# Decoder layer on one core: self-attention scores from float32r halves kept on chip, in place of bfloat16 triples stacked through HBM

## The reference, cut to what matters

```python
# x: (4, 512, 256), 16 heads of 16 columns
q, k, v = x @ w_q.T, x @ w_k.T, x @ w_v.T            # heads split off
scores = einsum('bqhd,bkhd->bhqk', q, k) * 16 ** -0.5
out = einsum('bhqk,bkhd->bqhd', softmax(scores), v)
x = layernorm(x + out @ w_o.T)
x = layernorm(x + cross_attention(x, ctx))           # 64 context rows a batch
x = layernorm(x + mixture_of_experts(x))             # 8 experts, 2 a token
```

## Time and profile before

| | us |
|---|---|
| median of three runs (888.09 to 890.46) | 890.4 |
| the profiled execution | 889.74 |
| its span, first to last instruction | 888.0 |
| busy in it: PE, PEld | 686.3, 449.1 |
| busy in it: DVE, ACT, POOL | 349.9, 285.8, 212.3 |

### The profile page before, as it was taken

The page is one execution under the profiler, slowest core; times in us unless marked ns, Lnnn a source line. Parts: engine busy times, 40 slices in busy tenths (PEclk is TensorE's granted clock), DMA queues, the critical chain, the costliest instruction groups (busy, mean ns, idle before and its releaser), DMA issues.

```text
span 888.0 us, 13256 instructions
## 1 busy us (share of the span) xinstructions
PE 686.3 (77%) x4099; PEld 449.1 (51%) x4100; DVE 349.9 (39%) x750; ACT 285.8 (32%) x501; POOL 212.3 (24%) x265
## 2 busy tenths in 40 slices
PE   7572266999999986764677862099999999999980
PEld 3230111322222245541213652089999999999970
DVE  2252344888888546653443875000000000000004
ACT  3220133767666643332354211011111111111112
POOL 1020100111111122112111067213333333333322
PEclk9876786999999999886689995599999999999995
DMA  6999992000001430858713722356666566656615
GB/s 207 129 170 169 141 151 32 3 1 1 1 1 44 136 53 37 134 82 130 98 53 101 250 77 50 105 161 180 175 169 177 167 173 180 174 174 175 170 45 189
DMA packets 75777, 103.61 MB, mean 117 GB/s; under 512 B 15044, under 2 KB 60637, under 8 KB 75742
## 3 DMA queue, kind: packets, MB, share of 16 engines
q1 hardware_dynamic: 63006, 90.53, 45.0%
q0 software_dynamic: 8512, 8.44, 5.8%
q10 hardware_dynamic: 4224, 4.19, 1.7%
HBM read 82.95 MB, written 21.40 MB: 118 GB/s over the span
## 4 chain that ended last, share of the span: by engine, by line
PE 64%; DMA 14%; DVE 7%; SPq 5%; POOL 4%; issue 3%; ACT 2%; DVEq 0%; ACTq 0%; POOLq 0%
PE ps L1566 16%; PE ps L1577 15%; PE ps L1288 7%; DMA scrq<-parts 7%; PE ps L1297 7%; PE ps L1233 5%; SPq L393 3%; POOL metas L664 3%; DMA qst<-mT 3%; PE ps L1381 2%; PE ps L1454 2%; PE ps L1447 2%; DMA qst<-scr_q 1%; PE ps L1413 1%; DVE xr L993 1%
## 5 line engine op out<-in xcount | busy, mean ns | idle before, releaser
L890 DVE TENSOR_REDUCE nmx<-ps 128x1 f32<-128x512 f32 x256 | 160.4, 681 | 55.0 <-PE ps L1233 55.0
L745 ACT ACTIVATE probs<-ps 128x512 f32<-128x512 f32 x256 | 133.8, 606 | 93.7 <-PE ps L1288 93.6
L1566 PEld LDWEIGHTS ps<-xtT,w1c 128*128 128x128 f32 x1248 | 147.1, 194 | 4.3 <-issue 2.4
L1566 PE MATMUL ps<-xtT,w1c 128*128 128x128 f32 x1248 | 147.6, 277 | 1.8 <-ACT xtT L845 1.8
L1577 PE MATMUL ps<-wexp,hidT 128*128 x624 | 141.0, 379 | 0.0
L1198 DVE TENSOR_SCALAR yw<-ps,mt 128x256 f32<-128x256 f32 x39 | 18.9, 484 | 292.2 <-PE ps L1577 292.2
L1577 PEld LDWEIGHTS ps<-wexp,hidT 128*128 128x128 f32 x624 | 115.6, 190 | 14.2
L1288 PE MATMUL ps<-qst,kst 99*128 (+1 forms) x256 | 96.4, 396 | 33.9 <-DMA qst<-mT 31.8
L1233 PE MATMUL ps<-kst,qst 96*128 (+1 forms) x256 | 94.6, 396 | 33.6 <-DVE nmx L890 17.3
L851 ACT ACTIVATE hidT<-ps 128x1024 f32<-128x1024 f32 x39 | 40.0, 1024 | 229.8 <-PE ps L1566 229.8
L703 POOL DMA_INDIRECT acc<-yw,mt x39 | 61.7, 1582 | 172.0 <-DVE yw L1198 172.0
(11 more groups left out here) (162 smaller groups left out, 668.1 us busy)
## 6 DMA issues: line engine op xcount, KB each, us to landing
w1c<-in_w1T SPq DMA_DIRECT2D x39, 1024.0 KB
wexp<-in_w2T SPq DMA_DIRECT2D x8, 1024.0 KB, 5.5
qst<-scrq SPq DMA_DIRECT2D x24, 256.0 KB, 9.2
kst<-scrk SPq DMA_DIRECT2D x24, 256.0 KB, 19.7
qst<-scr_q SPq DMA_DIRECT2D x24, 256.0 KB, 8.8
scrq<-parts SPq DMA_DIRECT2D x4, 768.0 KB, 18.1
scrk<-parts SPq DMA_DIRECT2D x4, 768.0 KB, 18.6
scr_q<-parts SPq DMA_DIRECT2D x4, 768.0 KB, 3.4
```

The lines of the kernel that those rows point to most:

```text
L745: act.activation(probs[n % 8][:, :], ps[:, 4 + n % 3, :], ACT.Exp).then_inc(s_exp, 1)
L890: dve.tensor_reduce(nmx[j % 2][:, k:k + 1], ps[:, slot, :], AX.X, ALU.max, negate=True).then_inc(s_mfree, 1)
L1566: mm = pe.matmul(ps[:, 2 * (j % 2) + f // 4, f % 4 * P:(f % 4 + 1) * P], w1c[j % 2][:, k * FF + f * P:k * FF + (f + 1) * P], xtT[j % 2][:, ...
```

## The change

Queries and keys are no longer split in bfloat16 triples. ScalarE evicts each projection to float32r (the high number), VectorE the rest (the low number), in tiles that stay on chip. To have high and low numbers of one head on 32 partitions, the weight columns are doubled first (`wqd`, `wkd`), so that a projection gives one unit's four heads on 4 x 32 partitions. A score tile is then two float32r matmuls on one row group of 32 rows of the array (32 rows, then 16, or 18 with the two rows of the maxima), and the four heads of a unit lie on the four row groups. Each projection has 128 columns, so there are 40 of them (16 for q, 16 for k, 8 for v), where the front had 12 larger ones; 33 of them now stand between score tiles, at places that two tables give. The whole of self-attention is written out, with no loop. Maxima run 26 tiles ahead of the exponentials (`LEAD`) and have three PSUM banks where they had four. They are turned as float32, copied as a high and a low number by VectorE, and moved into `qb` by eight DMAs a unit; two more DMAs a unit write ones. GpSimd has no part in the units any more, and `vu` is written by ScalarE at the eviction of v. The loads for later stages stand behind single units' rows on SP's queue.

```diff
+LEAD = 26
+TURN_AT = 3
+
+
+HIGHS = 2 * HD
+MAX_ROWS = 2
+PROJECTIONS = ("q0", "k0", "q1", "k1", "v0", "q2", "k2", "v1", "q3", "k3")
...
+    qa, qb, ka, kb = ([sb(f"{n}{i}", S, F32R, R_Q) for i in range(2 * NU)] for n in ("qa", "qb", "ka", "kb"))
...
+    PROLOGUE = {1: "q1", 4: "k1", 8: "v0", 12: "q2", 16: "k2"}
+    FIRST_BATCH_AT = {2: "v1", 6: "q3", 11: "k3"}
+    NEXT_BATCH_AT = [dict(zip(at, PROJECTIONS)) for at in
+                     ((15, 20, 25, 30, 35, 41, 46, 51, 57, 62), (3, 9, 17, 23, 29, 35, 41, 47, 53, 59))]
...
-        def make_stacks(b):
-            for qk in range(2):
-                sp.wait_ge(s_p3, 2 * b + qk + 1)
-                sp.dma_start(scr[qk][ds(b, 1)].rearrange("b (m p) r t -> p (b m) (r t)", p=P),
-                             parts[qk][:, :].rearrange("p (m a) -> p m a", m=KD)).then_inc(s_st[qk], 16)
-            sp.wait_ge(s_stack, 192 * b)
-            for qk, stack, part in ((0, qst, Q_PART), (1, kst, K_PART)):
-                sp.wait_ge(s_st[qk], 16 * (b + 1))
-                for g, r in enumerate(part):
-                    sp.dma_start(stack[HD * g:HD * g + HD, ds(b * H * S, H * S)].rearrange("d (h t) -> d h t", h=H),
-                                 scr[qk][ds(b, 1), :, r].rearrange("b (h d) t -> d (b h) t", d=HD)).then_inc(s_stack, 16)
...
+        def ones_rows(u):
+            sp.wait_ge(s_kb, u + 1)
+            for r in range(HD, HD + MAX_ROWS):
+                sp.dma_start(kb[u % (2 * NU)][r:P:HIGHS, :].bitcast(F32).rearrange("p (a t) -> p a t", a=HG),
+                             onesr[:, :].unsqueeze(1).to_broadcast([HG, HG, S // HG])).then_inc(s_one[u % NU], 16)
+
+        def max_rows(w):
+            sp.wait_ge(s_mfree, turn_slot(w) + 1)
+            for r, m in ((HD, mT_hi), (HD + 1, mT_lo)):
+                for i in range(HG):
+                    sp.dma_start(qb[w % (2 * NU)][HIGHS * i + r:HIGHS * i + r + 1, :].bitcast(F32).rearrange("p (a t) -> p a t", t=P),
+                                 m[w % 2][QT * i:QT * (i + 1), :].bitcast(F32)).then_inc(s_mrow[w % 2], 16)
...
+        ones_rows(0)
+        for w in range(UNITS):
+            if w + 1 < UNITS:
+                ones_rows(w + 1)
+            max_rows(w)
+            if w in BEHIND_ROWS:
+                BEHIND_ROWS[w]()
...
+        def q_high(b, u, name):
+            act.wait_ge(s_proj, proj_number(b, name) + 1)
+            act.activation(qb[(NU * b + u) % (2 * NU)][:, :], ps[:, proj_bank(b, name), :], ACT.Copy).then_inc(s_qb, 1)
...
+        for e in range(UNITS * TILES):
+            act.wait_ge(s_e, e + 1)
+            if e % HG == 0 and e >= 8:
+                act.wait_ge(s_pv, e // HG - 1)
+            act.activation(probs[e % 8][:, :], ps[:, 3 + e % 3, :], ACT.Exp).then_inc(s_exp, 1)
+            for b, name in projections_at(e):
+                evict(b, name)
...
+            dve.tensor_copy(mT_hi[w % 2][:, :], ps[0:TILES, n % 3, 0:P]).then_inc(s_mhi, 1)
+            dve.wait_ge(s_mhi, w + 1)
+            dve.tensor_tensor(mT_lo[w % 2][:, :], ps[0:TILES, n % 3, 0:P], mT_hi[w % 2][:, :], ALU.subtract).then_inc(s_mfree, 1)
...
+        def q_both(b, u, name):
+
+            n = NU * b + u
+            dve.wait_ge(s_qb, n + 1)
+            dve.scalar_tensor_tensor(out=qa[n % (2 * NU)][:, :], in0=ps[:, proj_bank(b, name), :], scalar=not_low[:, 0:1],
+                                     in1=qb[n % (2 * NU)][:, :], op0=ALU.mult, op1=ALU.add).then_inc(s_qa, 1)
+
+        def k_low(b, u, name):
+            n = NU * b + u
+            dve.wait_ge(s_ka, n + 1)
+            dve.tensor_tensor(kb[n % (2 * NU)][:, :], ps[:, proj_bank(b, name), :], ka[n % (2 * NU)][:, :],
+                              ALU.subtract).then_inc(s_kb, 1)
...
-        def max_half(w, k, j):
-
-            h, qt = k // QT, k % QT
-            n = max_tile(w, k)
-            if not (isinstance(w, int) and n < 4):
-                pe.wait_ge(s_mfree, n - 3)
-            pe.matmul(ps[:, tile_slot(j, k, isinstance(w, int) and w == 0), :],
-                      qst[0:ROWS, ds((w * HG + h) * S + qt * P, P)],
-                      kst[0:ROWS, ds((w * HG + h) * S, S)], start=True, stop=True).then_inc(s_mready, 1)
-
-        def max_turn(w, j, last=False):
-            pe.wait_ge(s_m3, w + 3)
-            pe.wait_ge(s_mfree, max_turned(w, last) - 3)
-            pe.transpose(ps[:, j % 4, :].bitcast(BF16)[0:M3W, 0:P], m3[j % 2][:, :], identb[:, :]).then_inc(s_mready, 1)
...
+        def max_tile(w, k):
+            n, (qt, i) = max_slot(w, k), divmod(k, HG)
+            if k == 0:
+                pe.wait_ge(s_qa, w + 1)
+                pe.wait_ge(s_kb, w + 1)
+            if n >= 3:
+                pe.wait_ge(s_mfree, n - 2)
+            u, both, highs = w % (2 * NU), slice(HIGHS * i, HIGHS * (i + 1)), slice(HIGHS * i, HIGHS * i + HD)
+            pe.matmul(ps[:, n % 3, :], qa[u][both, qt * P:(qt + 1) * P], ka[u][both, :], start=True, stop=False)
+            pe.matmul(ps[:, n % 3, :], qb[u][highs, qt * P:(qt + 1) * P], kb[u][highs, :], start=False,
+                      stop=True).then_inc(s_mready, 1)
+
+        def max_turn(w):
+            n = turn_slot(w)
+            pe.wait_ge(s_mfree, max(max_slot(w, TILES - 1) + 1, n - 2))
+            pe.matmul(ps[0:TILES, n % 3, 0:P], nmx[w % 2][:, :], identf[:, :], start=True, stop=True).then_inc(s_mready, 1)
...
+                    mm = pe.matmul(ps[:, at, :], wd[:, (k * NU + i) * P:(k * NU + i + 1) * P],
+                                   xTb[b][:, k * S:(k + 1) * S], start=(k == 0), stop=(k == KD - 1))
...
-        def exp_tile(u, n):
-            kt, h = n // HG, n % HG
-            if n >= 3:
-                pe.wait_ge(s_exp, HG * QT * u + n - 2)
-            pe.matmul(ps[:, 4 + n % 3, :], kst[:, ds((u * HG + h) * S + kt * P, P)],
-                      qst[:, ds((u * HG + h) * S, S)], start=True, stop=True).then_inc(s_e, 1)
...
+        def exp_tile(e):
+            u, (kt, i) = e // TILES, divmod(e % TILES, HG)
+            if e % TILES == 0:
+                pe.wait_ge(s_mrow[u % 2], 16 * HG * MAX_ROWS * (u // 2 + 1))
+                pe.wait_ge(s_one[u % NU], 16 * MAX_ROWS * (u // NU + 1))
+            if e >= 3:
+                pe.wait_ge(s_exp, e - 2)
+            w, both, more = u % (2 * NU), slice(HIGHS * i, HIGHS * (i + 1)), slice(HIGHS * i, HIGHS * i + HD + MAX_ROWS)
+            pe.matmul(ps[:, 3 + e % 3, :], ka[w][both, kt * P:(kt + 1) * P], qa[w][both, :], start=True, stop=False)
+            pe.matmul(ps[:, 3 + e % 3, :], kb[w][more, kt * P:(kt + 1) * P], qb[w][more, :], start=False,
+                      stop=True).then_inc(s_e, 1)
...
+        for e in range(UNITS * TILES):
+            exp_tile(e)
+            maxima(e + LEAD)
+            if e % HG == 1 and e >= HG:
+                pv(e // HG - 1)
+            for b, name in projections_at(e):
+                project(b, name)
```

519 lines of the change are left out of this document (232 added, 287 removed).

## The result

The changed kernel takes 930.5 us (924.6 to 937.6, 4 runs) against 890.4 (888.1 to 893.8, 4 runs) of the kernel before on the same chip: ratio 1.045, 95% interval 1.036 to 1.054. The forecast was 873 us with a range of 846 to 915. Faster was expected, slower came, and the range missed it.

A forecast was written before the change was run, and what follows sets the result against it. From 141 us TensorE was nearly always busy, units taking 11.93 us. Self-attention: 39.5 + 167.2 + 66 + 4.5 + 26.0 + 4.4 = 307.6 us against 324.4, so 889.7 - 16.8 = 873 us, range 846 to 915.

The forecast's parts named there:

- The clock: Rival: gaps at waits bring TensorE to 1.2 GHz for four of sixteen units, 44 us more, 917 us; chance 0.07.
- 0.216 a pass: Score tiles on TensorE: each float32r matmul is one 0.216 us pass, four side by side, 3.5 us a unit.
- A unit's base: Self-attention units: 11.94 us each without projections, as before, plus 0.3 for the float32 turn of the maxima.
- the last two: Last two units of self-attention, without maxima: taken as unchanged, 26.0 us.
- The start: Front up to the first maxima tile: doubled weights, projections q and k of unit 0, evictions; 12.5 us.
- GpSimd loses work that nobody waited for: nothing: Units: taking GpSimd's work away was priced at no time.
- Four groups side by side: Score tiles: four row groups work at once and a waiting group doesn't hold up the next; 873 us, chance 0.50.
- one pass for a float32r matmul: Score tiles: low numbers are split off beforehand, so a float32r matmul streams once, 0.216 us.
- 2.0 us a projection: 33 projections between score tiles: 1.71 us each plus two changes of array shape at 0.15, 66 us in all.
- waits for the maxima rows: Heads of units 12 to 15: TensorE waits 1.1 us each, 4.4 in all; batches 0 to 2 hide it.
- a granted clock below 0.9 between 40 and 300 us: Sign of wrongness in TensorE's clock column over the units; the sum assumed 2.4 GHz.
- The slack is used: Rival: TensorE's sum alone bounds units, 14.3 us with projections, 11.94 without; 826 us, halfway 848; chance 0.12.

The follow-up runs named there:

- after: The changed kernel itself, against the kernel before: 930.5 us, ratio 1.045; its profiled execution took 924.6 us.
- the fill: Changed kernel plus, from unit 12 on, two unread 128-row float32 identity matmuls ahead of every fourth exponential tile: 912.9 us.
- the changed kernel's second profile: The changed kernel repeated without edits beside the pair with fills: 923.9 us, the profiled execution 923.5 us.

## Why the prediction was wrong

Two steps failed, and one of them decides.

**The clock.** The sum priced everything behind q of unit 0 at 2.4 GHz: 1.9 us a projection in the prologue, 2.0 in the units, 0.216 a pass. The rival called "The clock" had a chance of 0.07, because the earlier trace rows show 2.4 GHz where TensorE is busy 99% of the time. That step failed: after has 1.2 GHz for 10 us with TensorE busy in all of them, behind 34 us in which it was busy for 32.8. What the runs showed in its place is that the busy share isn't enough and that the rows count: equal fills on 128 and on 32 rows of the array give 64.3 us at 1.00 and 74.3 us at 0.79 in the last four units, and 912.9 and 928.0 us for the whole, with no overlap of the executions. By this the change itself lowers the clock, since score matmuls on 16 to 32 of 128 rows replaced those on 96 and 99; this last link is argued and no run tests it by itself. Nor are the rows all: half a row maximum, with the same matmuls, had 0.97. And the rival's own reason, gaps at waits, has a part that isn't ruled out in the last units, where the falls of after came behind stretches with TensorE busy for 83 to 87%, as against 94% and more in units 0 to 11.

Its size, of the 54 us:

- ahead of the first maxima tile 1.9: k0 took 3.8 us for 1.9;
- from there to the first exponential tile 11.5: 38.5 us for 27.0 forecast. 8.2 of them are the five projections (four at 3.8 us for 1.9, that of v 2.6), 0.9 are not the clock but the eight DMAs of the maxima rows, which took 6.3 us for 5.4 (0.62 an issue for 0.53), and 0.4 are a slip of the sum (33.6 + 0.9 + 5.4 is 39.9, and it had 39.5). The other 2.0 weren't taken apart;
- units 0 to 11 12.3: 232.7 us for 212.9 forecast (12 x 11.94 + 33 x 2.0 + 12 x 0.3), less the 7.5 below. By the clock of the row, 0.94, 28 us lay at the low level and lost half, 14;
- units 12 to 15 9.0: 72.6 us to the start of the last copy for the 63.6 to the same point with the fill, where the clock is 1.00.

That is some 31 to 33 us; the division is worked out, from one execution. In the changed kernel's second profile it fell otherwise (50.6 us to the first exponential tile, 227.7 for units 0 to 11, 79.8 for the last four), with nearly the same sum.

**A unit's base.** Forecast 11.94 + 0.3, measured (107.2 - 30) / 6 = 12.9, 0.63 more, 7.5 us in 12 units. The mis-sized term is a score matmul, 0.33 us in a group of four and not 0.216. It doesn't act through TensorE's sum alone (in the unit without projections TensorE is busy for 12.0 of 14.3 us), but also through the round trips: half a row maximum on VectorE takes 0.9 us from a unit, a maxima tile of one matmul 0.3 to 0.8, and ScalarE idles for up to 1.3 us behind a `pv`. The same holds for the last four units: 63.6 us at the full clock for 55.2 forecast, 8.4 more. I had taken the last two from before, 26.0, as if two tiles cost the same without maxima tiles beside them. Two exponential tiles take 0.66 us where two bfloat16 passes took 0.43: 0.23 x 16 = 3.7 of the 8.4. The rest includes the fill of unit 15, and wasn't taken apart.

**The start.** 5.3 us late, and the rows above say how: k0 waited 2.4 us for VectorE's copy, q0 started 0.5 late and took 0.3 more than forecast, k0 ran at 1.2 GHz (the 1.9 above), the evictions took 0.2 more. The copy is a term that I had put at nothing: "GpSimd loses work that nobody waited for: nothing" was written without a look at what GpSimd gained, a memset that lengthened VectorE's operation.

5.3 (with k0's 1.9) + 11.5 + 12.3 + 9.0 + 7.5 + 8.4 = 54.0 us.

**What was right.** Four groups side by side without holding each other up; one pass for a float32r matmul; 2.0 us a projection; waits for the maxima rows only of 1 to 2 us, and only in few units (an unhidden 1.5 us at the head of a unit without projections, 1.1 forecast); 561 to 563 us behind the last copy. The signs of wrongness that I named included "a granted clock below 0.9 between 40 and 300 us", and that is what came in part: 0.5 from 40 to 62 us, 0.52 from 154 to 164, though 0.94 over units 0 to 11. The rival had priced it by four of sixteen units at the low level, 44 us; the runs have 31 to 33, spread otherwise. Its chance was off more than its price. Of the rivals, "The slack is used" fell: a projection costs its full 2.0.

## What to carry to other kernels

Before you replace matmuls on 99 rows by matmuls on 16 to 32 rows, price TensorE's other work at half speed too: here the float32 projections took 3.8 us for 1.9 wherever the clock was low. Look at the clock column of stretches in which TensorE is busy; busy 98% at 0.74 is a thing to find. If a stretch has waits, a few matmuls on the whole array inside them can be worth more than they cost (11 us less in the last units here), but not on the path (the version with a fill behind each maxima tile of the prologue gained nothing).

## What the hardware showed that I had not expected

- The granted clock can fall, and stay low, with TensorE busy throughout (32.8 of 34 us ahead of a fall, then 10.0 of 10.0 us at 0.52). With fewer rows in the projections three of four executions had 0.80 to 0.82 over the whole for 0.87 to 0.89, and the profiled one 0.73 for 0.89 over 370 us.
- Useless work made the kernel faster: 30 fill matmuls of 128 rows, 11 us less; the same on 32 rows, no gain.
- VectorE's second copy of 128 x 128 float32 into `wkd` took 4.7 us beside GpSimd's two memsets, and ended at 12.3 us, 0.5 behind them; with the memsets earlier it took 0.9. (The Trainium skill, "SBUF — State Buffer", "SBUF: two separate sides": VectorE and GpSimd share a port pair, and for some of VectorE's operations whichever starts first locks the other out until it has ended. The trace agrees in that the copy ended only behind the memsets.)
- Four score tiles of two matmuls each on four row groups take 0.66 us together. Where a group goes on behind them, its steps are 0.23 to 0.24 us (starts at 151.80, 152.03 and 152.27).
